# Loading half of the near table beside attention, and moving the input table's products to GpSimd, in a two-layer macaron kernel

## The chip, the cores and the metric

One core of a Trainium2 chip runs the whole program in one launch. The metric is the device time of that launch in microseconds (us). A core has TensorE (PE, with its weight loads shown apart as PEld), VectorE (DVE), ScalarE (ACT), GpSimd (POOL) and SyncE (SP, which here only issues DMAs). Each runs its own instructions in order and waits for the others by semaphores. All other data moves through 16 DMA engines.

## What is computed

x is 2048 rows of 128 numbers, f32. Six stages follow one another; `n` is a layer norm of the rows:

```python
x = x + 0.5 * moe8(n(x))                 # 8 experts, the best one for each row
x = x + windowed_attention(n(x))         # 16 heads, window of 32
x = x + 0.5 * moe8(n(x))
x = x + 0.5 * latent_block(x_normed)     # causal attention, then a moe of 4 experts
x = x + ssm(n(x))                        # state space layer
x = x + 0.5 * latent_block(x_normed)

def ssm(u):                              # D_MODEL 128, D_STATE 64, L = 2048
    K = einsum('mn,mln->ml', C_re, exp(dt[m] * A[n] * t[l]))
    return causal_convolution(u, K) + u * D

def moe(x, ...):                         # in the latent block
    top = argmax(x @ gate_w.T + gate_b)
    return (relu(x @ W1[top].T + b1[top]) @ W2[top].T + b2[top])
```

## The kernel before

The kernel is written by hand, engine by engine. The four MoE stages are numbered c = 0 to 3; c = 2 and c = 3 are those of the two latent blocks (B = 0 and B = 1), and they run the same code. "far" is True in block B = 0 alone: beside its own work it prepares the tables of the state space layer that comes next.

**A latent block.** `latent_prepare` makes keys and values. `latent_attention` runs a list of events that `plan` orders: 16 units (4 groups of 512 query rows times 4 pairs of heads); the last two units of group 3 come at places 8 and 9, those of group 2 at 10 and 11, then group 1, then group 0. `LAST[g]` is the last unit of group g. After its last unit, the group's queries (`split_q[g]`, 8 x 256 words for each partition from word 32 x 256 of `arena` on) are read no more. At the attention's end `leave_stage` drains all engines; there GpSimd scatters the 8 upper row tiles to `regions` (`scatter_routed`, one indirect DMA for each tile, L556). Then the 8 lower tiles ("late") are routed: DVE scales their rows (L1932), PE turns them (L1950), ACT copies (L1953), PE makes the gate's logits (L1957), DVE picks an expert for each row and works out its slot (`pick_dve` and `slots_dve`, a chain of small operations on 128 x 32 numbers, L410 to L441), and GpSimd scatters the 8 late tiles (L556). SP waits for all scatters to have landed, then loads 19 tiles of sorted rows (L535).

**The MoE over 19 tiles.** For each tile s, DVE copies the first layer's weights of the tile's expert to a fixed place (L661, two tiles ahead), PE multiplies (L598), ACT and DVE each make half of the hidden layer (L643 and L688), PE multiplies again (L608), DVE adds the bias (L668), and GpSimd scatters the tile's result to `made_rows` (L570). The next copy L661 waits for both halves of the tile. When all 19 have landed, SP loads the result back (L544), and the next stage's layer norm begins.

**The tables of the state space layer.** During attention of block 0, ACT and GpSimd make powers and products, PE sums them to 256 taps for each channel (event "states"), and SP writes them to `taps` in DRAM (semaphore `taps_out`, 256 when all are there). Two tables are left. `toep` (128 x 128 x 128, words 0 to 64 x 256 of `arena`, the near table) is loaded from `taps` in 8 DMAs of 1 MB (L2006), after the last row tile of the MoE has landed. `b_in` (128 x 128 x 64, words 64 x 256 to 96 x 256, where attention had its plain and shifted queries and its probabilities) is exp(-back x dt x A): in tiles s = 9 to 16 of the MoE, DVE multiplies a slice of 16 channels (128 x 1024 numbers, L1983) and ACT takes its exponential (L1998). At s = 7 ACT takes the exponentials of dt and A themselves (L1992, L1993), and DVE negates `back_col` (L1978). `state_space` reads `b_in` first, then `toep`.

## Times and profile before

| | us |
|---|---|
| three runs | 1702.85, 1703.96, 1698.28 |
| their median | 1702.85 |
| the profiled run: its time | 1704.4 |
| the profiled run: span from first to last instruction | 1703.1 |
| mean granted clock of TensorE, share of full speed | 0.847 |

| stage, in the profiled run | from, us | to, us |
|---|---|---|
| MoE of block 0 (c = 2), first hidden layer to the load back | 980.13 | 1038.36 |
| MoE of block 1 (c = 3), the same | 1648.57 | 1693.70 |

A row of the timeline has the start in us, the busy time in us, the engine, the line of the kernel, the operation, what it writes and reads, the count that was merged, and in brackets how long the engine was idle before it and who ended the idle time. Two rows with neighbouring starts may overlap a little, since an instruction is fetched while the one ahead ends. "psum" is the memory that TensorE writes, "arena" a large work area.

### The profile page before, as it was taken

The numbers are of one execution on the slowest core, as the hardware profiler recorded it, in microseconds if no ns is written. First come the engines' busy times: TensorE is split into PE (matmuls) and PEld (weight loads), VectorE is DVE, ScalarE is ACT, GpSimd is POOL, SyncE is SP. The second block draws the span as 40 slices with busy tenths as digits, with TensorE's granted clock in tenths as the row PEclk, the third lists the DMA queues.
The fourth block names the chain that finished last, engine by engine and source line by source line (L and its number), as shares of the span: only waits on it lengthen the run. The fifth ranks groups of instructions, "written<-read, shape, count | busy, mean of one in ns | idle before, by whom it ended". The sixth has DMA issues, their size and how long they took to land. (4 is left out here: it accounts for less than half of the span.)

```text
span 1703.1 us, 36518 instructions
## 1 busy us (share of the span) xinstructions
PE 1235.1 (73%) x13953; PEld 659.7 (39%) x13953; DVE 1175.8 (69%) x2641; ACT 945.3 (56%) x1507; POOL 570.0 (33%) x1034
## 2 busy tenths in 40 slices
PE   2664564447767788999997373877778999998756
PEld 2653454346542222223233273654222222233346
DVE  4348598625778989997873255476898999886234
ACT  1225775112345678878887241134566788888612
POOL 2431177045764321221112434375341111112333
PEclk9976665568579999999999596756999999999958
DMA  8410000022002100000000182000000000000022
GB/s 254 100 49 1 1 4 3 13 69 60 1 1 72 36 2 1 2 1 3 2 2 1 40 213 62 3 0 1 1 1 2 1 2 1 2 2 2 8 56 79
DMA packets 59134, 49.03 MB, mean 29 GB/s; under 512 B 7105, under 2 KB 54194, under 8 KB 58610
## 3 DMA queue, kind: packets, MB, share of 16 engines
q1 hardware_dynamic: 53282, 35.84, 7.9%
q0 software_dynamic: 4736, 9.74, 1.7%
q8 instruction: 114, 1.87, 0.5%
q10 hardware_dynamic: 944, 1.10, 0.2%
q14 instruction: 58, 0.48, 0.1%
HBM read 32.72 MB, written 18.38 MB: 30 GB/s over the span
## 5 line engine op out<-in xcount | busy, mean ns | idle before, releaser
L1808 DVE TENSOR_REDUCE arena<-psum 128x1 f32<-128x512 f32 (+4 forms) x1152 | 680.8, 656 | 138.7 <-PE psum L1619 97.6
L1751 ACT ACTIVATE arena<-psum 128x1024 f32<-128x1024 f32 (+3 forms) x640 | 558.1, 900 | 179.8 <-PE psum L1641 170.7
L1657 PE MATMUL psum<-arena 128*9 128x256 f32 (+2 forms) x4352 | 338.3, 387 | 0.9 <-POOL arena L1868 0.8
L1619 PE MATMUL psum<-arena 64*128 64x128 bf16 (+3 forms) x1664 | 223.1, 316 | 94.7 <-DVE arena L1808 87.0
L1641 PE MATMUL psum<-arena 64*128 64x512 bf16 (+3 forms) x1280 | 227.7, 356 | 23.3 <-ACT arena L1751 16.1
L1868 POOL TENSOR_SCALAR_AFFINE_SELECT arena<-arena 128x256 f32<-128x256 f32 x256 | 103.4, 408 | 367.9 <-ACT arena L1751 364.8
L1619 PEld LDWEIGHTS psum<-arena 64*128 64x128 bf16 x1664 | 69.2, 95 | 270.9 <-DVE arena L1808 233.2
L1641 PEld LDWEIGHTS psum<-arena 64*128 64x128 bf16 x1280 | 62.9, 94 | 175.9 <-ACT arena L1751 78.6
L1657 PEld LDWEIGHTS psum<-arena 128*9 128x9 f32 x4352 | 67.5, 88 | 151.8 <-issue 117.5
L1846 POOL CAST arena<-arena 128x16 bf16<-128x16 f32 x64 | 16.4, 257 | 283.9 <-DVE arena L1813 281.8
L688 DVE TENSOR_SCALAR small<-psum,YT 128x128 f32<-128x128 f32 x168 | 50.6, 343 | 77.7 <-PE psum L598 76.8
L643 ACT ACTIVATE small<-psum,YT 128x128 f32<-128x128 f32 x168 | 52.5, 364 | 84.7 <-PE psum L598 77.5
L598 PE MATMUL psum<-arena,YT 128*128 128x128 f32 x672 | 97.6, 293 | 0.1
L598 PEld LDWEIGHTS psum<-arena,YT 128*128 128x128 f32 x672 | 88.2, 205 | 3.0 <-issue 1.6
L1756 ACT ACTIVATE arena<-psum 128x1024 bf16<-128x1024 bf16 x64 | 65.4, 1024 | 33.9 <-PE psum L1605 33.3
L589 PE MATMUL psum<-ident,ACCn 128*128 128x128 f32 x16 | 7.2, 469 | 89.9 <-DMA ACCn<-sorted_rows 57.6
L570 POOL DMA_INDIRECT made_rows<-arena,index x38 | 42.5, 1120 | 77.5 <-DVE arena L668 75.8
L556 POOL DMA_INDIRECT sorted_rows<-Yn,slot x32 | 31.3, 978 | 81.3 <-DVE slot L374 72.2
L608 PE MATMUL psum<-w,small 128*128 x304 | 43.9, 290 | 15.5 <-ACT small L643 13.1
L608 PE MATMUL psum<-big_w,small 128*128 x368 | 50.9, 283 | 0.4 <-issue 0.4
L632 ACT ACTIVATE arena<-psum 128x128 f32<-128x128 f32 (+2 forms) x18 | 7.9, 444 | 77.5 <-PE psum L589 69.5
L570 POOL DMA_INDIRECT made_rows<-arena,ACCn x32 | 31.0, 968 | 56.2 <-DVE arena L668 56.2
(357 smaller groups left out, 2011.5 us busy)
## 6 DMA issues: line engine op xcount, KB each, us to landing
arena<-taps SPq DMA_DIRECT2D x8, 1024.0 KB
big_w<-in_w SPq DMA_DIRECT2D x2, 2048.0 KB, 19.3
ACCn<-made_rows SPq DMA_DIRECT2D x16, 256.0 KB, 3.8
regions<-sorted_rows SPq DMA_DIRECT2D x5, 741.8 KB, 4.6
sorted_rows<-arena SPq DMA_DIRECT2D x2, 1483.5 KB, 13.9
ACCn<-regions SPq DMA_DIRECT2D x32, 64.5 KB, 1.8
w<-in_w SPq DMA_DIRECT2D x2, 1024.0 KB
ACCn<-sorted_rows SPq DMA_DIRECT2D x6, 258.0 KB, 3.0
```

Of the source, the lines that this page charges most:

```text
L570: pool.indirect_dma_start(made_rows, bass.IndirectOffsetOnAxis(to, 0), made[q % 2][:, s % GT, :], None).then_inc(rows_made[q % 2], 16)
L598: mm = pe.matmul(hidden_of(s, k), first[s % 2][:, k * P:(k + 1) * P], xt[s // GT % 2][:, (s % GT) * P:(s % GT + 1) * P], start=True, stop= ...
L608: mm = pe.matmul(psum[:, 4 + s % 2, 0:D], hid[s % 2][:, k, :], flat2[:, bass.ds(expert[s] * HID + k * P, D)], start=(k == 0), stop=(k == H ...
L643: half = act.activation(hid[s % 2][:, k, :], hidden_of(s, k), ACT.Relu, bias=first[s % 2][:, HID + k:HID + k + 1])
L688: half = dve.tensor_scalar(hid[s % 2][:, k, :], hidden_of(s, k), first[s % 2][:, HID + k:HID + k + 1], 0.0, ALU.add, ALU.max)
L1619: mm = pe.matmul(psum[:, bank_of(("max", (v, m + r))), at:at + w], plain_q[v % 2][rows, a, i * P:(i + 1) * P], keys[rows, 2 * hq + a, key: ...
L1641: mm = pe.matmul(psum[:, b + r, off:GW], keys[rows, 2 * hq + a, t * P:(t + 1) * P], shift_q[v % 2][rows, a, off:GW], start=True, stop=True)
L1657: mm = pe.matmul(psum[32 * hh:32 * hh + 9, O_BANK, lo:hi], values[:, tile_of(v, j), 4 * hq + hh, :], prob[(t + hh // 2) % N_PROB][:, hh % ...
L1751: act.activation(prob[t % N_PROB][:, :, off:GW], both, ACT.Exp, scale=INV_SQRT_HD).then_inc(a_got, 1)
L1756: act.activation(dst, bank.bitcast(BF16).rearrange("p (a t) -> p a t", a=2), ACT.Copy).then_inc(a_got, 1)
L1808: dve.tensor_reduce(place, rows, AX.X, ALU.max).then_inc(a_max_got, 1)
L1868: pool.affine_select(out=part, in_=part, compare_op=ALU.is_ge, fill=0.0, base=0, pattern=[[0, 2], [1, P]], channel_multiplier=-1).then_inc ...
```

## The change

- **The near table.** Its upper half (channels 64 to 127, which lies where `split_q` was) is loaded beside attention in 16 DMAs of 256 KB: four for each group, from group 3 down to 0, each after a score of the group's last unit has been read. The lower half is loaded as before, in 4 DMAs of 1 MB.
- **The other table's products.** The 8 multiplications go from DVE (tiles 9 to 16) to GpSimd: two after `scatter_routed`, ahead of the late scatters, and six behind these. ACT takes the exponential of the first two behind the routing's copies, and of the other six behind tiles 1 to 6 of the MoE. The exponentials of dt and A go to the start of attention on ACT, the negation of `back_col` to its start on DVE.
- **Eight products that nobody reads.** In both blocks PE makes 8 products of 128 x 512 bf16 into a free bank of psum, ahead of turning the late rows.

```diff
+        def keep_warm(bank, n):
+            for _ in range(n):
+                pe.matmul(psum[:, bank, :].rearrange("p (a k) -> p a k", k=P), identb[:], counts[:].unsqueeze(1).broadcast_to([P, GT, P]),
+                          start=True, stop=True)
...
                     act.activation(alog_col[:], alog_col[:], ACT.Exp).then_inc(pair_made, 1)
+                    act.wait_ge(rates_in, 32)
+                    act.activation(logdt_all, logdt_all, ACT.Exp).then_inc(pair_made, 1)
+                    act.activation(alog_all, alog_all, ACT.Exp).then_inc(pair_made, 1)
...
+                if far:
+                    dve.tensor_scalar(neg_back[:], back_col[:], -1.0, None, ALU.mult).then_inc(neg_made, 1)
...
                 sp.wait_ge(taps_out, 256)
+                for g in range(NG - 1, -1, -1):
+                    for k in range(GT):
+                        sp.wait_ge(a_got, act_base + number["score", (LAST[g], k, 0)] + 1)
+                        near_table_sp(D // 2 + STEP * g + STEP // GT * k, STEP // GT)
...
+        def near_table_sp(m, n):
+            sp.dma_start(toep[:, m:m + n, :], bass.AP(tensor=taps.tensor, offset=m * 2 * P, ap=[[1, P], [2 * P, n], [1, P]])).then_inc(toep_in, 16)
+        NEAR = [slice(STEP * k, STEP * k + STEP) for k in range(D // STEP)]
+        def near_rates(k):
+            pool.wait_ge(pair_made, 4)
+            pool.wait_ge(taps_out, 256)
+            pool.tensor_tensor(b_in[:, NEAR[k], :], bcast(logdt_all[:, NEAR[k]], NS), alog_all.unsqueeze(1).broadcast_to([P, STEP, NS]),
+                               ALU.mult).then_inc(near_made, 1)
+        def near_grown(k):
+            act.wait_ge(near_made, k + 1)
+            act.wait_ge(neg_made, 1)
+            act.activation(b_in[:, NEAR[k], :], b_in[:, NEAR[k], :], ACT.Exp, scale=neg_back[:, 0:1]).then_inc(near_exp, 1)
...
             latent_attention(B, far, n, c)
+            if far:
+                for k in range(2):
+                    near_rates(k)
...
             scaled_rows(LATE)
+            keep_warm(5, 8)
...
             scatter_pool(c, 1, LATE, ACCn, regions)
+            if far:
+                for k in range(2):
+                    near_grown(k)
+                for k in range(2, D // STEP):
+                    near_rates(k)
...
-                if far and s == 7:
-                    dve.tensor_scalar(neg_back[:], back_col[:], -1.0, None, ALU.mult).then_inc(neg_made, 1)
-                    dve.wait_ge(rates_made, 3)
-                    dve.wait_ge(taps_out, 256)
-                if far and 0 <= s - 9 < D // STEP:
-                    m = STEP * (s - 9)
-                    dve.tensor_tensor(b_in[:, m:m + STEP, :], bcast(logdt_all[:, m:m + STEP], NS),
-                                      alog_all.unsqueeze(1).broadcast_to([P, STEP, NS]), ALU.mult).then_inc(near_made, 1)
...
             def beside_act(s):
-                if far and s == 7:
-                    act.wait_ge(rates_in, 32)
-                    act.activation(logdt_all, logdt_all, ACT.Exp).then_inc(rates_made, 1)
-                    act.activation(alog_all, alog_all, ACT.Exp).then_inc(rates_made, 1)
-                    act.wait_ge(neg_made, 1)
-                if far and 0 <= s - 9 < D // STEP:
-                    part = b_in[:, STEP * (s - 9):STEP * (s - 8), :]
-                    act.wait_ge(near_made, s - 8)
-                    act.activation(part, part, ACT.Exp, scale=neg_back[:, 0:1]).then_inc(near_exp, 1)
+                if far and 2 <= s + 1 < D // STEP:
+                    near_grown(s + 1)
...
                 sp.wait_ge(tile_in[CHUNKS[c] - 1], tiles_in(c, CHUNKS[c] - 1))
-                for m in range(0, D, STEP):
-                    dst, src = toep_in_of(m)
-                    sp.dma_start(dst, src).then_inc(toep_in, 16)
+                for m in range(0, D // 2, STEP):
+                    near_table_sp(m, STEP)
...
-                pe.wait_ge(toep_in, 16 * 8)
+                pe.wait_ge(toep_in, 16 * (D // 2 // STEP + NG * GT))
```

GpSimd (POOL) between attention and MoE in block 0, before: the last mask of attention, the scatters of the upper tiles, those of the late tiles, and the first rows made by the MoE.

```order
L1868 AFFINE_SELECT arena<-arena 128x2x128 [waits a_got] x13
L556 DMA regions<-ACCn,slot 8576x129 [waits slots_made,regions_in]
L556 DMA regions<-ACCn,slot 8576x129 x7
L556 DMA regions<-ACCn,slot 8576x129 [waits slots_made,stage_left]
L556 DMA regions<-ACCn,slot 8576x129 x7
L570 DMA made_rows<-arena,index 4992x128 [waits row_made,index_set]
```

The same place after; `window_mask` and `bo` are the places where dt and A lie for all partitions.

```order
L1879 AFFINE_SELECT arena<-arena 128x2x128 [waits a_got] x13
L562 DMA regions<-ACCn,slot 8576x129 [waits slots_made,regions_in]
L562 DMA regions<-ACCn,slot 8576x129 x7
L1956 TENSOR_TENSOR arena<-window_mask,bo 128x1024 [waits taps_out,pair_made,stage_left]
L1956 TENSOR_TENSOR arena<-window_mask,bo 128x1024 [waits taps_out,pair_made]
L562 DMA regions<-ACCn,slot 8576x129 [waits slots_made]
L562 DMA regions<-ACCn,slot 8576x129 x7
L1956 TENSOR_TENSOR arena<-window_mask,bo 128x1024 [waits taps_out,pair_made] x6
L576 DMA made_rows<-arena,index 4992x128 [waits row_made,index_set]
```

Two multiplications stand ahead of the late scatters, and six between these and the MoE's first scatter.

VectorE (DVE) in one of the tiles 9 to 16 of the MoE of block 0, before; L661 writes the next weights (here named by the place, YT), L688 makes half a hidden layer.

```order
L661 ISA [waits hid_act,layer1_made]
L661 COPY YT<-w 128x516
L668 ISA [waits rows_made0,layer2_made]
L668 TENSOR_TENSOR arena<-psum,arena 128x128
L1983 TENSOR_TENSOR arena<-window_mask,bo 128x1024
L688 TENSOR_SCALAR small<-psum,YT 128x128 [waits layer2_made,layer1_made]
```

The same tile after.

```order
L667 ISA [waits hid_act,layer1_made]
L667 COPY YT<-w 128x516
L674 ISA [waits rows_made0,layer2_made]
L674 TENSOR_TENSOR arena<-psum,arena 128x128
L694 TENSOR_SCALAR small<-psum,YT 128x128 [waits layer2_made,layer1_made]
```

The multiplication is gone from the tile, and nothing has come in its place.

TensorE (PE) at the end of attention in both blocks, before: the output's projection (wo), the late rows turned, and the gate.

```order
L1721 MATMUL psum<-wo,YT 128x128 x3
L1950 MATMUL psum<-ident,ACCn 128x128 [waits o_rows,stage_left]
L1950 MATMUL psum<-ident,ACCn 128x128 x3
L1950 MATMUL psum<-ident,ACCn 128x128 [waits o_rows]
L1950 MATMUL psum<-ident,ACCn 128x128 x3
L1957 MATMUL psum<-gate,YT 128x4 [waits fm_copied]
```

The same place after.

```order
L1727 MATMUL psum<-wo,YT 128x128 x3
L187 MATMUL psum<-counts,identb 128x512 [waits stage_left]
L187 MATMUL psum<-counts,identb 128x512 x7
L1988 MATMUL psum<-ident,ACCn 128x128 [waits o_rows]
L1988 MATMUL psum<-ident,ACCn 128x128 x3
L1988 MATMUL psum<-ident,ACCn 128x128 [waits o_rows]
```

The eight unread products begin as soon as the stage is left, and the turning of the late rows stands behind them.

## Rows read from the trace of the kernel before

**Rows 1.** Windows: busy us (x instructions) PE, PEld, DVE, ACT, POOL; clock; DMA; GB/s.
```profile
1005.00:1010.00 5.00, 2.19 (x18) 1.86 (x16) 3.04 (x8) 3.30 (x6) 2.77 (x2) 1.00 1.18 302
```

**Rows 2.** Timeline, ACT and SP: first hidden layer and load back, blocks 0 and 1.
```profile
980.13 0.63 ACT L643 ACTIVATE small<-psum,YT 128x128 f32<-128x128 f32 x2 [1.34 <-PE psum L598]
...
1038.36 2.01 SPq L544 DMA_DIRECT2D ACCn<-made_rows  x4
...
1648.57 0.63 ACT L643 ACTIVATE small<-psum,YT 128x128 f32<-128x128 f32 x2 [1.34 <-PE psum L598]
...
1693.70 2.03 SPq L544 DMA_DIRECT2D ACCn<-made_rows  x4
```

**Rows 3.** Timeline, DVE: one tile of block 0's MoE, then one of block 1's.
```profile
1007.69 1.22 DVE L1983 TENSOR_TENSOR arena<-window_mask,bo 128x1024 f32<-128x1024 f32 x1
...
1011.36 1.22 DVE L1983 TENSOR_TENSOR arena<-window_mask,bo 128x1024 f32<-128x1024 f32 x1
...
1675.98 0.43 DVE L661 COPY YT<-w 128x516 f32 x1 [0.84 <-PE psum L598]
...
1677.97 0.43 DVE L661 COPY YT<-w 128x516 f32 x1 [0.84 <-PE psum L598]
```

**Rows 4.** Groups by shape, POOL over the span: busy us, mean ns, idle before.
```profile
L1861 POOL TENSOR_TENSOR big_w<-big_w,c_pair 128x2064 f32<-128x2064 f32 x4 | 14.5, 3636 | 0.3
...
L774 POOL TENSOR_TENSOR arena<-arena,qk_w 128x512 f32<-128x512 f32 x4 | 7.0, 1754 | 62.2 <-DVE arena L868 62.2
...
L2028 POOL TENSOR_TENSOR X<-X,ACCn 128x2048 f32<-128x2048 f32 x1 | 4.2, 4168 | 0.1
```

**Rows 5.** Timeline, DVE and POOL between attention and MoE, block 0.
```profile
957.36 0.19 DVE L412 TENSOR_TENSOR small<-small 128x32 f32<-128x32 f32 x1
957.59 0.19 DVE L413 TENSOR_TENSOR small<-small,order 128x32 f32<-128x32 f32 x1
...
959.48 0.17 DVE L441 CAST slot<-small 128x8 uint32<-128x8 f32 x1
...
981.65 0.43 DVE L661 COPY YT<-w 128x516 f32 x1 [0.84 <-DVE small L688]
...
960.43 0.96 POOL L556 DMA_INDIRECT regions<-ACCn,slot  x1 [5.01 <-DVE slot L441]
...
984.92 0.96 POOL L570 DMA_INDIRECT made_rows<-arena,index  x1 [14.57 <-DVE arena L668]
```

**Rows 6.** Timeline, POOL and DVE at once, in windowed attention and after the state space.
```profile
270.27 1.27 POOL L1034 TENSOR_TENSOR arena<-arena 128x512 f32<-128x512 f32 x1
...
270.58 1.50 DVE L1003 TENSOR_TENSOR arena<-arena 128x512 f32<-128x512 f32 x1
...
1094.73 0.98 POOL L1513 MEMSET arena<- 128x1024 bf16 x1
1094.81 0.92 DVE L1473 TENSOR_SCALAR scales<-meanvar 128x4 f32<-128x4 f32 x1
```

**Rows 7.** Timeline of PE, three places, and a window in the columns of rows 1.
```profile
526.51 1.04 PE L1605 MATMUL psum<-identb,arena 128*128 128x128 bf16 x8
...
910.86 1.28 PE L1711 MATMUL psum<-gate,YT 128*128 128x4 f32 x10
...
1620.26 1.94 PE L1950 MATMUL psum<-ident,ACCn 128*128 128x128 f32 x8 [4.14 <-DVE ACCn L1932]
1622.12 3.57 PE L1957 MATMUL psum<-gate,YT 128*128 128x4 f32 x16
...
1646.62 3.62 PE L598 MATMUL psum<-arena,YT 128*128 128x128 f32 x16
...
1648.00:1653.00 5.00, 5.00 (x29) 5.00 (x29) 2.26 (x8) 1.26 (x4) 0.00 (x0) 0.58 0.25 63
```

**Rows 8.** Timeline, ACT: the exponential of dt, and block 1's first step after attention.
```profile
997.36 0.31 ACT L1992 ACTIVATE window_mask<-window_mask 128x128 f32<-128x128 f32 x1
...
1618.76 0.21 ACT L1943 ACTIVATE rstd<-rstd 128x8 f32<-128x8 f32 x1 [0.52 <-ACTq L177]
```

2 lines of the change are left out of this document (removed).

## The prediction, made before the changed kernel was run

> **What bounds the kernel now.** No engine is the bound throughout, so I read the two MoE stages of the latent blocks side by side. They run the same code on 19 tiles, except that the first also prepares the state space layer's tables. From the first hidden layer to the load back, block 0 takes 1038.36 - 980.13 = 58.2 us and block 1 takes 1693.70 - 1648.57 = 45.1 us [rows 2]. The table work costs 13.1 us there. The timeline of DVE tells where: with a multiplication L1983 (1.22 us) in it, a tile lasts 1011.36 - 1007.69 = 3.67 us, in block 1 1677.97 - 1675.98 = 1.99 us [rows 3]. Eight such tiles differ by 8 x 1.68 = 13.4 us, which is the whole 13.1. The multiplication explains 1.2 of the 1.7; the rest is that ACT's exponential waits for it, and the next weight copy waits for ACT. It isn't TensorE: in such a stretch it is busy 2.19 of 5 us at clock 1.00 [rows 1].
>
> **The tiles lose the multiplications: -13.1 us.** What block 1 takes is what block 0 should take without table work on DVE. The DMAs are not in it: in the same window they move 302 GB/s [rows 1], and no tile's 3.67 us is more than its DVE and ACT work explains. The DMA half that stays (4 MB, 14 us at that rate) is issued where the whole was, and is in long before the stage ends; the half beside attention is issued by SP, which has nothing else to do there, and DMAs take no engine's time. I cost both at 0. If a transfer were late, PE would wait for it ahead of the near products; of that there is no sign.
>
> **Six exponentials stay on ACT, in tiles 1 to 6: +0.2.** Of the new tiles' period of 2 us, the two activations L643 take 0.63 [rows 2], an exponential at most 1.22, L1983's time for the same width [rows 3]. 1.85 fits. In tiles 2 and 6 ACT also copies the next rows and may overrun a period a little. The first two exponentials fall where ACT has nothing to do. The negation on DVE is one tiny operation, and is costed at 0.
>
> **Two exponentials at attention's start: +0.35.** The first ACT copy there waits behind them. That of dt takes 0.31 [rows 8], but the next begins 0.2 after its start; the other is smaller. Bounds 0 (if PE was late anyway) and 0.5.
>
> **The price of a multiplication on GpSimd** isn't in the trace, so it is bounded: 3636 / 2064 x 1024 = 1.8 us by L1861, 1754 x 2 = 3.5 us by L774, which goes in runs of 8 elements; by L2028, 4168 / 2 = 2.1 us [rows 4]. The new one has runs of 64, nearer to L1861 and L2028. I take 2.0. The Trainium skill (GPSIMD Engine Reference, section on elementwise cycle accounting) has 4497 ns for 2048 elements, an estimate of 2.25 us for ours; the sum below would be about 1.2 us worse by it, and the row of this kernel decides.
>
> **Two multiplications ahead of the late scatters: +2.2.** GpSimd is idle for 5.01 us before the first late scatter at 960.43 [rows 5], so since 955.42. The two run to about 955.6 + 2 x 2.05 = 959.7, and the slots come at 959.48 + 0.17 = 959.65. By this alone they just fit. But DVE's routing runs at the same time, and rows 6 show what happens then: DVE's L1003 begins at 270.58 with GpSimd's L1034 running until 270.27 + 1.27 = 271.54, and takes 1.50 us, though its 512 columns at L1983's rate (1024 in 1.22) need about 0.6. So it waited for the end of GpSimd's instruction, and then went ahead of GpSimd's next one. In the routing L412 (957.36) and L413 (957.59) both read two operands from SBUF, as L1003 does [rows 5]. L412 would wait until 957.65, L413 behind the second multiplication until 959.75. From L413 to the slots it is 959.65 - 957.59 = 2.06, so the slots come at 961.8, late by 2.2. All that follows (scatters, landing, loads, MoE) moves by it. Bounds: 0 without such waiting, +3.1 at 2.5 us each. What PE adds ahead of L412 in this block (below) is covered up to 1.4 us, since L412 would be waiting then anyway.
>
> The Trainium skill (SBUF — State Buffer, section on the two separate sides) states the same as a rule: DVE and GpSimd share one pair of ports, held by one instruction at a time, against DVE operations in a 2-port mode or with two inputs from SBUF. It speaks against placing these products beside the routing; hanging on it are the +2.2 and the +1.0 below, and without both the sum would be -12.4.
>
> **Six multiplications behind the late scatters: +1.0.** Today these scatters end at 984.92 - 14.57 = 970.35 [rows 5]; now 972.6. Six more take until 972.6 + 6 x 2.05 = 984.9. The MoE's own first GpSimd scatter is due at 984.92 + 2.2 = 987.1, so no row waits. DVE's third weight copy L661 is due at 981.65 + 2.2 = 983.9 [rows 5], while the last multiplication runs. A DVE operation with one input waits too: L1473, four numbers, took 0.92 us beside a GpSimd memset that began at 1094.73 and lasted 0.98 [rows 6]. The copy waits some 1.0 us, and since DVE paces these tiles, that stays. Bounds 0 and 2.8 (at 2.5 us each, two or three waits).
>
> **Eight unread products: +0.1 in block 1, nothing more in block 0.** PE is free once the stage is left, just before 1618.76, when ACT gets its release [rows 8]: say 1618.55. Today it waits until 1620.26 for the scaled rows [rows 7]. Eight bf16 products of 128 columns took 1.04 us at the lower level [rows 7], about 0.11 each; ours have 512 columns, 0.44 each, 3.5 in all, until 1622.05. The turning is late by 1.8. Against this stands the clock. From 1646.62 on PE multiplies densely (16 x L598 in 3.62 us), and the mean of 0.58 in 1648 to 1653 says that the clock went from half (1.2 GHz) to full (2.4 GHz) near 1652.2, so 5.6 us later [rows 7]. Counted from 1618.55 that is 1624.1, when the gate's 16 products L1957 would just begin. They took 3.57 us at half; ten of the same shape took 1.28 at full (L1711), so 16 take 1.9 [rows 7]: 1.7 us back. Net +0.1. Bounds -0.5 (the clock rises earlier) and +1.8 (it doesn't rise in time).
>
> **The sum.** -13.1 + 0.2 + 0.35 + 2.2 + 1.0 + 0.1 = -9.25 us. The profiled run took 1704.4, so it would be 1695.2. The median of the three runs is 1702.85 (1698.28 to 1703.96); less 9.25 it gives 1693.6, my forecast.
>
> **The rivals.**
> - *No waiting between DVE and GpSimd.* The routing's operations are very short, and the copy may come between two products. Then 2.2 and 1.0 go: -12.4, 1690.4. Rows 6 speak against it.
> - *The unread products only delay.* The clock rises by what PE did before, and the turning is all that follows them; the gate's products have 4 columns. Then +1.8 in block 1 instead of +0.1; block 0 hides most of it. -7.5, 1695.3. Speaks for it: the margin between 1624.1 and the end of dense work is nil.
> - *GpSimd is slower, 2.5 us each:* the routing costs 3.1, the MoE 2.8. -6.5, 1696.3.
> - *Slower than before: GpSimd's products last into the MoE.* At 3.5 us each (L774's price) the two cost the routing 2 x 3.55 - 1.9 = 5.2, and the six end at 975.6 + 21.3 = 996.9, while the MoE starts its hidden layers at 985.3. If DVE gets nothing done in those 11.6 us, the sum is -13.1 + 0.2 + 0.35 + 5.2 + 11.6 + 1.8 = +6, 1708.9. With x for the price it is about 8x - 22.2 in this worst case, so it decides from x = 2.8 on.
> - *The change doesn't do what it says:* block 1 is no measure, since something else (the load's traffic, or the exponentials in the early tiles) holds the tiles, and half the gain stays away: -9.25 + 6.5 = -2.7, 1700.1.
>
> **How the numbers follow.** Forecast 0.50; no waiting 0.14; unread products only delay 0.17; slower GpSimd 0.09; half the gain 0.05; slower 0.05. The range goes from below the first rival (1689.5) to 1699.5, above the cases of -7.5 and -6.5 with room for the before runs, whose own spread is 5.7 us; it leaves out half the gain and the slower case, and the tails. 0.3% is 5.1 us, about what a measurement of this kernel can tell from no change. The first four cases, 0.90, lie beyond it, but the two smaller gains by little, so I give faster 0.83, within 0.3% 0.13, slower 0.04.
>
> **What would show it.** In the profile after: block 0's stage near 46.5 us; tiles 9 to 16 at 2.0 us on DVE; the product on GpSimd near 2.0; L412 and L413 of the routing (with new line numbers) longer than 0.19, and the late scatters some 7.2 us behind the earlier ones' end instead of 5.0; one weight copy of DVE near the MoE's start longer than 0.43; the gate's 16 products in block 1 near 1.9 us, or 3.6 if the clock didn't rise. Wrong it would be if tiles 9 to 16 stayed above 2.5 us, or a wait for `toep_in` or `near_exp` showed up in the state space stage.

## The result: faster by 0.83%, more than forecast

| | before | after |
|---|---|---|
| median, us (8 runs each) | 1702.13 | 1690.65 |
| lowest and highest, us | 1698.28, 1708.98 | 1685.82, 1692.31 |
| ratio of the runs, 95% interval | | 0.9917 (0.9902 to 0.9933) |

By the ratio the change takes off 14.1 us (11.4 to 16.7), where 9.25 were forecast; the difference of the medians is 11.5. Three later controls gave ratios of 0.9920, 0.9925 and 0.9891. The kernel is faster, as forecast, but by more than the sum said, and by the ratio more than the range allowed (from 1702.85 it reached down to 1689.5, so 13.35 us).

The profiled run after took 1690.99 us (span 1689.7). First both MoE stages, ACT and SP, the rows that answer to [rows 2]:

```profile
986.07 0.63 ACT L649 ACTIVATE small<-psum,YT 128x128 f32<-128x128 f32 x2 [1.34 <-PE psum L604]
...
1030.69 2.01 SPq L550 DMA_DIRECT2D ACCn<-made_rows  x4
...
1635.96 0.63 ACT L649 ACTIVATE small<-psum,YT 128x128 f32<-128x128 f32 x2 [1.34 <-PE psum L604]
...
1680.72 2.03 SPq L550 DMA_DIRECT2D ACCn<-made_rows  x4
```

Block 0's MoE takes 1030.69 - 986.07 = 44.6 us instead of 58.2, and block 1's 44.8. DVE in two tiles of block 0, at the place of [rows 3]: the multiplication is gone and a tile lasts 1006.77 - 1004.78 = 1.99 us.

```profile
1004.78 0.43 DVE L667 COPY YT<-w 128x516 f32 x1 [0.85 <-ACT small L649]
1005.13 0.28 DVE L674 TENSOR_TENSOR arena<-psum,arena 128x128 f32<-128x128 f32 x1
1005.33 0.60 DVE L694 TENSOR_SCALAR small<-psum,YT 128x128 f32<-128x128 f32 x2
1006.77 0.43 DVE L667 COPY YT<-w 128x516 f32 x1 [0.84 <-PE psum L604]
```

Between attention and MoE of block 0, DVE and GpSimd (POOL), at the place of [rows 5]:

```profile
959.13 0.96 POOL L562 DMA_INDIRECT regions<-ACCn,slot  x1 [0.30 <-issue]
959.56 0.19 DVE L416 TENSOR_TENSOR small<-psum,gateb 128x32 f32<-128x32 f32 x1 [3.69 <-PE psum L1995]
959.78 0.19 DVE L417 TENSOR_REDUCE small<-small 128x8 f32<-128x32 f32 x1
960.00 3.93 DVE L418 TENSOR_TENSOR small<-small 128x32 f32<-128x32 f32 x1
960.11 3.76 POOL L1956 TENSOR_TENSOR arena<-window_mask,bo 128x1024 f32<-128x1024 f32 x2
...
963.97 0.19 DVE L419 TENSOR_TENSOR small<-small,order 128x32 f32<-128x32 f32 x1
...
966.31 1.01 POOL L562 DMA_INDIRECT regions<-ACCn,slot  x1 [2.43 <-DVE slot L447]
...
976.38 11.18 POOL L1956 TENSOR_TENSOR arena<-window_mask,bo 128x1024 f32<-128x1024 f32 x6
...
987.60 0.43 DVE L667 COPY YT<-w 128x516 f32 x1 [0.84 <-DVE small L694]
```

L418 (L412 before) takes 3.93 us instead of 0.19: it ends when both multiplications have ended, at 963.87. The next one, L419, waits for nothing. From the end of the last upper scatter (959.13 + 0.96 = 960.09) to the first late one it is 6.22 us, where it was 5.01. A multiplication takes 11.18 / 6 = 1.86 us. The six end at 987.56, and DVE's third weight copy comes at 987.60 and takes 0.43.

TensorE in block 1's routing, and the two exponentials at attention's start on ACT, which answer to [rows 7] and [rows 8]:

```profile
1606.54 3.52 PE L187 MATMUL psum<-counts,identb 128*128 128x512 bf16 x8 [2.20 <-ACTq L177]
1609.89 1.04 PE L1988 MATMUL psum<-ident,ACCn 128*128 128x128 f32 x8
1611.28 1.95 PE L1995 MATMUL psum<-gate,YT 128*128 128x4 f32 x16 [0.34 <-ACT YT L1991]
```

```profile
492.15 0.29 ACT L1747 ACTIVATE window_mask<-window_mask 128x128 f32<-128x128 f32 x1
492.35 0.24 ACT L1748 ACTIVATE bo<-bo 128x64 f32<-128x64 f32 x1
492.50 1.00 ACT L1765 ACTIVATE arena<-psum 128x1024 bf16<-128x1024 bf16 x1
```

After the unread products the turning takes 1.04 us instead of 1.94 and the gate's products 1.95 instead of 3.57.

One profile each doesn't settle where the gain lies, since stages with the same code differ between executions too. With the experiments' controls there are three profiles of the kernel before and four of the changed one. The borders are: ACT's first exponential at attention's start (L1738 before, L1744 after), ACT's square root for the late rows (L1943, L1980), the first hidden layer, and the load back.

| stage | before, mean (range) | after, mean (range) | difference |
|---|---|---|---|
| ahead of attention of block 0 | 491.0 (489.6 to 492.8) | 491.3 (489.9 to 493.6) | +0.3 |
| attention of block 0 | 459.5 (458.2 to 461.3) | 461.0 (458.9 to 462.3) | +1.5 |
| routing of block 0 | 30.75 (30.55 to 31.05) | 31.85 (31.19 to 32.34) | +1.1 |
| MoE of block 0 | 58.33 (58.22 to 58.55) | 44.78 (44.49 to 45.31) | -13.55 |
| load back of block 0 to late routing of block 1 | 580.42 (580.40 to 580.46) | 578.62 (576.33 to 579.99) | -1.8 |
| routing of block 1 | 29.79 (29.76 to 29.81) | 29.05 (28.94 to 29.24) | -0.74 |
| MoE of block 1 | 45.05 | 44.89 | -0.2 |
| the rest | 9.8 | 9.1 | -0.7 |
| span | 1704.7 | 1690.6 | -14.0 |

The MoE and the routing of block 0, the routing of block 1, and attention's first copy (+0.3) give -12.9 us. The rest of attention, beside which the 16 DMAs now run, is not in this sum: its +1.5 is less than what it varies in one kernel (458.2 to 461.3 before).

### The profile page after: what moved, and what is told of

Its sections match the earlier page's. It is cut to its first block and busy times, and to the rows that moved or that the text cites. A ratio compares the mean times of both kernels' runs of the same rounds, so it can differ in the third digit from the quotient of the medians.

```text
span 1689.7 us, 36574 instructions
## 1 busy us (share of the span) xinstructions
PE 1233.8 (73%) x13969; PEld 655.1 (39%) x13969; DVE 1169.9 (69%) x2633; ACT 945.2 (56%) x1507; POOL 578.8 (34%) x1042
## 5 line engine op out<-in xcount | busy, mean ns | idle before, releaser
L694 DVE TENSOR_SCALAR small<-psum,YT 128x128 f32<-128x128 f32 x168 | 50.5, 342 | 77.4 <-PE psum L604 76.6
L604 PE MATMUL psum<-arena,YT 128*128 128x128 f32 x672 | 97.3, 293 | 0.7 <-issue 0.6
L604 PEld LDWEIGHTS psum<-arena,YT 128*128 128x128 f32 x672 | 87.6, 205 | 4.5 <-issue 2.7
L576 POOL DMA_INDIRECT made_rows<-arena,index x38 | 37.6, 990 | 57.1 <-DVE arena L674 54.9
L614 PE MATMUL psum<-big_w,small 128*128 x368 | 51.0, 283 | 0.5 <-issue 0.5
L667 DVE COPY YT<-big_w 128x516 f32 x46 | 21.2, 461 | 39.4 <-PE psum L604 27.1
```

Source lines behind the costliest of these rows:

```text
L576: pool.indirect_dma_start(made_rows, bass.IndirectOffsetOnAxis(to, 0), made[q % 2][:, s % GT, :], None).then_inc(rows_made[q % 2], 16)
L604: mm = pe.matmul(hidden_of(s, k), first[s % 2][:, k * P:(k + 1) * P], xt[s // GT % 2][:, (s % GT) * P:(s % GT + 1) * P], start=True, stop= ...
L614: mm = pe.matmul(psum[:, 4 + s % 2, 0:D], hid[s % 2][:, k, :], flat2[:, bass.ds(expert[s] * HID + k * P, D)], start=(k == 0), stop=(k == H ...
L694: half = dve.tensor_scalar(hid[s % 2][:, k, :], hidden_of(s, k), first[s % 2][:, HID + k:HID + k + 1], 0.0, ALU.add, ALU.max)
```

## The experiments

**Theory:** the gain is the multiplications' move off DVE; against it stands the routing's wait behind GpSimd; the DMAs are free; the unread products bring the clock up earlier. **Rivals:** the early DMAs or the moved exponentials carry part of the gain; the routing isn't held by GpSimd; the unread products only delay. A ratio below is that to the kernel before on the same chip, with its 95% interval.

### Three controls

The changed kernel twice and the kernel before once, unedited.

> The changed kernel once more, as a control for the others and for stages whose code is the same in both kernels. In the two profiles shown, the part from block 0's load back to block 1's first step after attention, whose instructions are identical, takes 580.40 us before and 576.33 after. Theory (the clock's steps fall elsewhere in each execution): here the same part takes some other value between 573 and 583 us, the time differs from the first profile's, and the stages that the change touches repeat: routing of block 0 about 32.3 us, MoE of block 0 about 44.6 us, DVE's second-operand instruction L418 again near 3.9 us. Rival (the change itself makes the later part faster, by what it leaves in memory or queues): the part takes 576.3 again within 0.5 us.

> The kernel before once more. Its first profile had 580.40 us from block 0's load back to block 1's first step after attention, while five profiles of changed kernels have 579.02, 579.02, 579.04, 578.82 and 576.33 us with the same instructions there. Theory (this part differs by where the clock's steps fall, not by the change): a value between 576 and 582, not systematically above 579; MoE of block 0 again 58.2 us, routing of block 0 30.5, of block 1 29.8. Rival (the change makes that part shorter by 1.4 us in each execution): 580.4 again.

> The changed kernel once more, beside the two that follow, so that they can be compared on one chip. Stages of the two profiles before: routing of block 0 32.34 and 32.00 us, MoE of block 0 44.62 and 44.71, routing of block 1 28.94 and 29.07. Expected: the same within 0.4 us, DVE's L418 between 1.9 and 3.95 us long, by when it comes in the row of two multiplications.

Measured: 1691.27 us, 0.9920 (0.9901 to 0.9939), and 1691.67 us, 0.9925 (0.9912 to 0.9938), for the changed kernel; 1706.16 us, 1.0002 (0.9991 to 1.0013), for the one before. The touched stages repeat (table above). The wait is there again, but shorter than the 3.9 us that I had expected, since DVE comes later in the row of two, in after_again:

```profile
956.18 0.19 DVE L416 TENSOR_TENSOR small<-psum,gateb 128x32 f32<-128x32 f32 x1 [5.17 <-PE psum L1995]
956.41 0.19 DVE L417 TENSOR_REDUCE small<-small 128x8 f32<-128x32 f32 x1
956.63 1.99 DVE L418 TENSOR_TENSOR small<-small 128x32 f32<-128x32 f32 x1
...
954.78 3.77 POOL L1956 TENSOR_TENSOR arena<-window_mask,bo 128x1024 f32<-128x1024 f32 x2
```

The first multiplication ends at 954.78 + 1.88 = 956.66. DVE asks at 956.63, 0.03 us ahead of that, and still waits until the second has ended. So close to the border that alone proves little; but in after_third L418 starts at 958.96, 0.9 us ahead of the border, and ends at 961.82 with the second (958.00 + 3.76 = 961.76). L417, a reduction with one input from SBUF, takes its 0.19 us in the midst of the row.

### The multiplications back on DVE in tiles 9 to 16 (tiles_on_dve)

```diff
-                for k in range(2):
-                    near_rates(k)          # GpSimd, ahead of the late scatters
...
-                for k in range(2, D // STEP):
-                    near_rates(k)          # GpSimd, behind them
...
+                if far and 0 <= s - 9 < D // STEP:
+                    near_rates(s - 9)      # on DVE, in tile s
```

> The changed kernel with the eight multiplications back on DVE in tiles 9 to 16 of the MoE, the exponentials behind them as before; the exponentials of dt and A at attention's start, half of the near table beside attention and the unread products stay as changed. Theory (the gain is the multiplications' move alone): MoE of block 0 58.2 us (tiles at 3.67), routing of block 0 30.5 us, so 13.6 - 1.5 = 12 us slower than the changed kernel and within 1 us of the kernel before. Rival (part of the 13.6 us is from the DMAs moved out of the MoE, or from the exponentials of dt and A moved out): MoE at 52 to 57 us.

Measured: MoE of block 0 58.47 us, routing of block 0 31.09, routing of block 1 29.14; 1704.77 us, 0.9993 (0.9981 to 1.0005). All of the MoE's gain is gone, though half of the near table still comes beside attention and the exponentials of dt and A are still early. DVE at the place of [rows 3]:

```profile
1012.44 0.43 DVE L667 COPY YT<-w 128x516 f32 x1 [1.38 <-ACT small L649]
1012.78 0.28 DVE L674 TENSOR_TENSOR arena<-psum,arena 128x128 f32<-128x128 f32 x1
1012.98 1.22 DVE L1956 TENSOR_TENSOR arena<-window_mask,bo 128x1024 f32<-128x1024 f32 x1
1014.12 0.61 DVE L694 TENSOR_SCALAR small<-psum,YT 128x128 f32<-128x128 f32 x2
1016.11 0.43 DVE L667 COPY YT<-w 128x516 f32 x1 [1.38 <-ACT small L649]
```

A tile is 3.67 us again. The early DMAs alone gain nothing.

### The whole near table loaded in the MoE (table_whole)

```diff
-                for g in range(NG - 1, -1, -1):
-                    for k in range(GT):
-                        sp.wait_ge(a_got, ...)
-                        near_table_sp(D // 2 + STEP * g + STEP // GT * k, STEP // GT)
...
-                for m in range(0, D // 2, STEP):
+                for m in range(0, D, STEP):
```

> The changed kernel with the whole near table loaded in the MoE, as before, and nothing of it beside attention. In the kernel before, eight DMAs kept 300 GB/s up for 27 us from about 998 on, and ended 11 us ahead of the load back. In the changed kernel the load back comes 13.6 us sooner, so the eight would end about when it begins, 1 to 2 us behind it. Theory (the split is worth nothing on its own and 1 to 3 us once the MoE is short): attention the same, MoE tiles at 2.0 to 2.1 us as in the changed kernel, MoE of block 0 44.7 us, and 1 to 3 us more from the load back to the states' products, since the loaded rows land later. Rival (the prediction's 0 for all of it): no stage differs by more than 0.5 us. Rival (the split disturbs attention or the whole load slows the MoE's tiles): attention shorter by over 1 us than 458.3 us, or tiles above 2.2 us.

Measured: MoE of block 0 47.58 us, 3.1 more than after_third on the same chip (44.49), all tiles alike (first to last 38.95 us against 38.91), attention the same (462.3 both, so the 16 DMAs beside it cost nothing there); 1693.99 us, 0.9935 (0.9920 to 0.9949). By the timed runs alone this isn't to be told from the changed kernel; the stage is. The end of the MoE on GpSimd, whose last scatter of results must land ahead of the load back, here and in after_third:

```profile
1028.55 0.96 POOL L576 DMA_INDIRECT made_rows<-arena,index  x1 [0.30 <-issue]
1033.88 0.21 POOL L2041 MEMSET arena<- 128x64 f32 x1 [4.37 <-DMA made_rows<-arena,index]
```

```profile
1026.24 0.95 POOL L576 DMA_INDIRECT made_rows<-arena,index  x1 [0.30 <-issue]
1028.53 0.21 POOL L2046 MEMSET arena<- 128x64 f32 x1 [1.33 <-DMA made_rows<-arena,index]
```

The wait for the landing is 4.37 us with the table and 1.33 without, 3.04 more, which is the 3.1. Windows of table_whole in the columns of rows 1 show the table still moving there, at 320 and 294 GB/s:

```profile
1027.00:1030.00 3.00, 0.26 (x3) 0.07 (x1) 0.29 (x1) 0.23 (x1) 1.92 (x2) 1.00 1.15 320
1030.00:1033.00 3.00, 0.00 (x0) 0.00 (x0) 0.00 (x0) 1.06 (x1) 0.00 (x0) 0.90 1.02 294
```

So the theory had the cost right and the place wrong: not the loaded rows, but the last results land late. The split is worth 0 in the long MoE (tiles_on_dve) and 3.0 us in the short one. The Trainium skill (DMA: Bandwidth & Descriptors, section on queues, rings and completion order) says that a DMA engine takes its queues in turn, packet by packet. The landing that comes 3 us later, while another queue is busy, agrees in direction; how the turns fall no run here shows.

### Without the unread products (no_unread)

```diff
-            keep_warm(5, 8)
```

> The changed kernel without the eight unread products, in both blocks. Theory: they are worth 0.9 us in block 1's routing (28.94 us with them, 29.81 in the kernel before), and nothing in block 0, where DVE's L418 waits until 963.9 for GpSimd whatever TensorE does; so slower by about 0.9 us, the gate's 16 products of block 1 at 3.6 us instead of 1.95, and block 0's routing at 32.3 as with them. Rival (they only delay the turning): faster by 1.8 us. Rival (they bring the clock up in block 0 as well, which matters): slower by 2.5 us.

Measured: routing of block 1 29.76 us, of block 0 32.07, 1693.91 us, 0.9929 (0.9910 to 0.9947). TensorE in block 1:

```profile
1607.01 1.94 PE L1987 MATMUL psum<-ident,ACCn 128*128 128x128 f32 x8 [4.13 <-DVE ACCn L1966]
1608.87 3.57 PE L1994 MATMUL psum<-gate,YT 128*128 128x4 f32 x16
```

Block 1 loses 0.7 us, as in the kernel before; block 0 is as in after_again (32.00). The rival that they only delay falls. The timed runs can't tell 0.7 us.

### All eight multiplications behind the late scatters (all_behind), and the same with waits (behind_apart)

```diff
-            if far:
-                for k in range(2):
-                    near_rates(k)
...
-                for k in range(2, D // STEP):
+                for k in range(D // STEP):
+                    if k:                            # behind_apart alone
+                        pool.wait_ge(near_made, k)   # behind_apart alone
                     near_rates(k)
```

> The changed kernel with all eight multiplications on GpSimd behind the late scatters, none ahead. Theory (L418's 3.93 us was its wait for both multiplications, and the whole routing waited with it): the late scatters start about 3.7 us earlier after the earlier ones' end, the routing of block 0 takes 28.6 us instead of 32.3. The eight then run for 8 x 1.87 = 15 us and end some 5 us after the MoE's first hidden layer. If DVE waits for the whole row of multiplications, its third weight copy loses 3.8 us and the sum is 0; if it comes in between two of them, two copies or so lose 1 us each, and the sum is -2. Rival (the routing wasn't held by that wait): no gain in the routing, and 1 to 4 us slower in all.

> As the run with all eight multiplications on GpSimd behind the late scatters, but GpSimd waits for each multiplication's own semaphore before it starts the next. There DVE's third weight copy took 4.00 us, to the end of the last multiplication, and the MoE 50.4 us. Theory (a row of GpSimd multiplications that follow each other without a wait keeps DVE out as a whole; a wait between them lets DVE in): no DVE instruction waits longer than 2.0 us, the third weight copy takes 0.4 to 2.3 us, the MoE of block 0 46 to 48 us, so 2.5 to 4 us faster than that run and about as fast as the changed kernel or 1 us better. Rival (DVE is kept out as long as GpSimd has multiplications, wait or not): the copy again takes until the last one ends, MoE 50.4.

Measured for all_behind: routing 29.89 us, MoE 50.40; 1693.44 us, 0.9927 (0.9911 to 0.9942). For behind_apart: routing 30.94, MoE 47.41; 1693.64 us, 0.9925 (0.9907 to 0.9943). From DVE's first routing step (L416) to the first late scatter it is 3.5 us in both, as in the kernel before; with two multiplications ahead it is 6.75, 4.81, 5.69 and 4.57 us in the four profiles of the changed kernel. So the wait does hold the routing, though without it the routing took 29.89 us and not the 28.6 expected. all_behind, DVE beside the row of eight:

```profile
973.06 14.91 POOL L1956 TENSOR_TENSOR arena<-window_mask,bo 128x1024 f32<-128x1024 f32 x8
...
982.80 0.61 DVE L694 TENSOR_SCALAR small<-psum,YT 128x128 f32<-128x128 f32 x2 [13.12 <-PE psum L604]
984.25 4.00 DVE L667 COPY YT<-w 128x516 f32 x1 [0.84 <-DVE small L694]
```

behind_apart, the same place:

```profile
972.94 15.83 POOL L1956 TENSOR_TENSOR arena<-window_mask,bo 128x1024 f32<-128x1024 f32 x8
...
984.15 0.89 DVE L667 COPY YT<-w 128x516 f32 x1 [0.84 <-PE psum L604]
984.95 1.86 DVE L683 COPY_PREDICATED index<-valid,ACCn 128x4 uint32<-128x4 uint32 x1
```

The copy L667 waits 3.6 us, until the last of the row ends at 987.97. With GpSimd waiting for its own semaphore between two multiplications (0.13 us each: (15.83 - 14.91) / 7), the copy comes in after at most one, and nothing takes longer than 1.86. The theory of the row holds, with a limit: no wait in these runs goes past more than one border between two multiplications, so that a longer row holds DVE to its end isn't shown. L694, which reads psum, takes its 0.61 us beside the multiplications in both. Neither version wins: against the changed kernel's means all_behind gains 2.0 us in the routing and loses 5.6 in the MoE, behind_apart gains 0.9 and loses 2.6.

The 5.6 us are more than the wait of 3.6. TensorE has nothing to do meanwhile (3.19 us idle), and when it goes on its granted clock is at half (a window in the columns of rows 1):

```profile
988.30:992.10 3.80, 3.75 (x17) 3.78 (x18) 1.99 (x8) 0.63 (x2) 1.01 (x1) 0.50 0.23 53
```

Eight products L614 ahead of the idle time took 1.06 us; eight L604 behind it take 2.05, in after_again 1.06 at a granted clock of 1.00 (983.30 to 987.40). By the starts of DVE's half of the hidden layer, the second and third tile together last 2.1 us longer than in after_again, which is the rest.

### The multiplications in DVE's idle time (gap_on_dve, gap_three, gap_three_four)

DVE is idle for 13 us between the routing's tables and the first hidden layer (the 13.12 in brackets in all_behind's rows). GpSimd issues a tiny memset behind its last late scatter, on whose semaphore DVE starts:

```diff
+                pool.memset(scattered_mark[:], 0.0).then_inc(pair_made, 1)
+                for k in range(NEAR_EARLY):          # 6; 3 in gap_three
+                    near_grown(k)
...
+            def ahead_dve():                         # called behind the first two weight copies
+                for k in range(D // STEP):
+                    near_rates(k)                    # on DVE, waits for pair_made 5
...
-            keep_warm(5, 8)
+            keep_warm(5, 4)                          # gap_three_four and gap_four_second alone
```

> The changed kernel with all eight multiplications on DVE, in its 13 us of idle time between the routing's tables and the first hidden layer, behind a mark that GpSimd sets after its last late scatter; six exponentials follow at once on ACT, two go into tiles 1 and 2 of the MoE. Theory: the late scatters start 3.7 us earlier, eight multiplications at 1.22 to 1.24 us take 9.9 us, from the mark at about 972.5 to 982.4, and the first hidden layer is due at about 982.4: 3.7 us faster than the changed kernel, routing 28.6 us, MoE 44.6. Rival (the routing wasn't held by the wait): no difference. Rival (DVE's multiplications last into the MoE): 1 to 2 us of the 3.7 are lost.

> As the run with the multiplications in DVE's idle time, but with three of the exponentials ahead of the MoE's row copies on ACT instead of six, five in tiles 1 to 5. There the routing took 31.85 us, 1.1 more than pick at 7.34 us and late scatters 3.5 us behind it would give, and ACT's first row copy came at +28.9 us of it instead of +25.5, behind the sixth exponential. Theory (ACT's row copies waited for the exponentials): first row copy at +25.5, routing 30.5 us, MoE 44.6 to 44.9, so 1.3 us faster than that run and 1.5 us faster than the changed kernel. Rival (something else holds the first hidden layer, as the loads of the sorted rows): routing stays at 31.8.

> The run with the multiplications in DVE's idle time and three exponentials ahead of the MoE's copies, with four unread products in each block in place of eight. In block 1 eight took 3.5 us at half clock and put the turning off from +1.50 to +2.86 us behind ACT's step, while the gate's 16 products fell from 3.57 to 1.95 us; the pick came at +6.22 instead of +6.97. Theory (four end at about +1.3, ahead of the scaled rows, and put nothing off; the clock has then risen or not): if it has risen when the gate's products come, pick at +5.4 to +5.8 in block 1, 0.5 to 0.8 us sooner than with eight; if not, at +6.97, 0.75 us later. I expect the latter in one of two executions, so no difference in the time. Block 0: routing 30.1 to 30.6 us, MoE 44.6 to 44.9; about 1.5 us faster than the changed kernel on the same chip.

gap_on_dve: routing 31.85 us, MoE 44.48; 1689.74 us, 0.9908 (0.9891 to 0.9925). gap_three: routing 30.11, MoE 44.60; 1690.49 us, 0.9922 (0.9899 to 0.9944). gap_three_four: 30.11, 44.27, and 28.33 in block 1's routing; 1686.22 us, 0.9887 (0.9873 to 0.9902), beside 0.9925 of the changed kernel on the same chip. The routing of 28.6 us that I expected of gap_on_dve didn't come, and gap_three's 1.5 us over the changed kernel can't be told in its time. DVE and ACT in gap_on_dve:

```profile
971.28 9.17 DVE L1961 TENSOR_TENSOR arena<-window_mask,bo 128x1024 f32<-128x1024 f32 x8 [3.50 <-POOL scattered_mark L2005]
972.54 6.82 ACT L1967 ACTIVATE arena<-arena,neg_back 128x1024 f32<-128x1024 f32 x6 [15.88 <-DVE arena L1961]
...
979.27 0.60 ACT L641 ACTIVATE arena<-psum,norm_w 128x128 f32<-128x128 f32 x2
```

Eight multiplications take 9.17 us and end at 980.45, ahead of the first hidden layer. But ACT's first row copy stands behind the sixth exponential. With three ahead of it, the copy comes in time (gap_three):

```profile
972.96 3.42 ACT L1967 ACTIVATE arena<-arena,neg_back 128x1024 f32<-128x1024 f32 x3 [14.99 <-issue]
976.40 0.37 ACT L641 ACTIVATE arena<-psum,norm_w 128x128 f32<-128x128 f32 x1
```

Four unread products, in block 1 of gap_three_four:

```profile
1606.53 1.89 PE L187 MATMUL psum<-counts,identb 128*128 128x512 bf16 x4 [2.20 <-ACTq L177]
1608.41 1.73 PE L1989 MATMUL psum<-ident,ACCn 128*128 128x128 f32 x8
1610.31 1.95 PE L1996 MATMUL psum<-gate,YT 128*128 128x4 f32 x16 [0.17 <-ACT YT L1992]
```

They put nothing off, and the gate's products still run at 1.95 us. I had expected that in one of two executions. In block 0 of the same execution it went the other way: the four ran at full clock, and the gate's products behind them at half.

```profile
953.15 1.04 PE L187 MATMUL psum<-counts,identb 128*128 128x512 bf16 x4 [2.20 <-ACTq L177]
...
956.95 3.58 PE L1996 MATMUL psum<-gate,YT 128*128 128x4 f32 x16
```

The granted clock there is 0.50 from 955 to 960.6. So four are not enough everywhere.

### Once more, for what was open

before_third and after_fourth are the two kernels, gap_three_second and gap_four_second the last two versions, all unedited.

> The kernel before, for the part with identical instructions. Theory (it differs by where the clock's steps fall, and two values of 580.4 were chance): below 580.0 or above 580.9. Rival (the change shortens it by 1.4 us or more): 580.4 within 0.4. The touched stages: routing of block 0 30.5 to 31.1 us, MoE of block 0 58.2 to 58.6, routing of block 1 29.8.

> The changed kernel, control for this chip. The part with identical instructions took 576.33, 579.02 and 579.14 us; theory (the clock's steps): any value between 576 and 581; rival (shortened by the change): 579.1 or below. Touched stages: 32.0, 44.6, 29.0 us.

> Multiplications in DVE's idle time, three exponentials ahead of the MoE's copies, eight unread products. Routing of block 0 30.1 us against 32.0, MoE 44.6: 1.9 us faster than the changed kernel by the stages. The first time the timed runs showed 0.9922 against 0.992 and 0.9925 of the changed kernel, thus nothing, with one run of 1699.6 among six. Theory (the stages are right, that comparison was across chips): 1.5 to 2.5 us faster than after_fourth. Rival (the gain is given back later): the same time as after_fourth.

> The same with four unread products in each block. Its first profile had block 1's pick at +5.29 us behind ACT's step instead of +6.22 and the routing at 28.33 us instead of 29.0. Theory (four end ahead of the scaled rows, put nothing off and still bring the clock up): block 1's pick again at +5.3 to +5.6, 0.7 us faster than gap_three_second, 2.5 to 3.5 us faster than after_fourth. Rival (it was that execution's luck where the clock stepped): pick at +6.9, no faster than gap_three_second.

| | median, us | ratio (95% interval) | routing 0 | MoE 0 | routing 1 |
|---|---|---|---|---|---|
| before_third | 1705.56 | 0.9996 (0.9982 to 1.0011) | 30.66 | 58.22 | 29.76 |
| after_fourth | 1688.54 | 0.9891 (0.9867 to 0.9916) | 31.19 | 45.31 | 29.24 |
| gap_three_second | 1690.87 | 0.9904 (0.9885 to 0.9923) | 30.77 | 45.92 | 29.65 |
| gap_four_second | 1689.08 | 0.9893 (0.9873 to 0.9913) | 30.73 | 45.10 | 28.13 |

Block 1's routing with four products repeats (28.33, 28.13; with eight 28.94 to 30.45 in eleven profiles; without 29.76 to 29.81 in four): DVE's first step (the "pick" of the expectations) comes 5.29 us behind ACT's both times, instead of 6.21 to 6.58 and 6.97 to 7.13. So four are worth 1.5 us in block 1, in two of two profiles, and eight 0.7 in the changed kernel (0.5 over all eleven). In time the version with four beats the changed kernel on one chip (by 5.5 us of the medians) and not on the other; by the three stages it is 2.6 and 1.8 us faster. gap_three_second missed its expectation: 1.5 to 2.5 us faster than after_fourth, it came out 2.3 us slower by the medians and 0.6 by the three stages. gap_four_second was to be 2.5 to 3.5 us faster and was 0.5 slower by the medians. That it beats both kernels is shown against the kernel before, and only likely against the changed one.

The part with identical instructions took 580.46 us in before_third and 579.99 in after_fourth. Three profiles before lie within 0.06 us, and all fourteen of changed kernels below them (576.33 to 579.99). before_again (580.41) and before_third are where the rival had them; after_fourth is above the 579.1 that it wanted. So the rival, that something shortens this part a little, has more for it than my theory of chance, but less than three equal numbers suggest: before_again is 4.0 us behind the first profile from 194 to 525 us into the part (by the same copies of ACT) and has made it all up by the end. No run names the cause: it stays without the unread products (579.02), with the whole table in the MoE (579.38) and with the multiplications back on DVE (577.37).

## Why the prediction was right in kind and too small in size

The cause was right: the gain is the multiplications' move off DVE, and GpSimd's take a part of it back. Three steps of the sum failed, all to the same side. The wait ahead of the late scatters was put at +2.2 and cost +1.1. The wait of the third weight copy was put at +1.0 and didn't come, by a margin of 0.04 us. The unread products were put at +0.1 and gave 0.74 back, since the clock was already up for the turning, and not only for the gate's products. Against each step, the means of the table:

- **Tiles lose the multiplications, -13.1.** Right, and the largest term: tiles_on_dve returns it whole. With the next two steps the forecast for the stage was -11.9; it was -13.55. Tiles 9 to 16 together went from 29.3 us (before) to 16.7 (after_again), by the starts of DVE's half of the hidden layer; the other 1.0 lies in the first tiles and the stage's end. Of the 1.65 us that the stage gained beyond the forecast 1.0 is the copy's wait below and 0.2 the exponentials; the last 0.45 is within what the stage varies (44.49 to 45.31).
- **The DMAs at 0.** The sum's 0 came out only because the table was split. Block 1, my measure for the tiles, has no table load, so its 45.1 us hold no landing behind one; the step asked whether PE waits for the table, and not who waits behind it once the MoE ends 13 us sooner. Without the split 3.0 of the 13.55 stay away (table_whole).
- **Exponentials in tiles, +0.2:** about nothing; tiles 1 to 6 last as long as in block 1.
- **Two exponentials at attention's start, +0.35:** right for the copy. The copy started 490.88 - 490.61 = 0.27 us behind the first exponential before, and starts 492.50 - 491.90 = 0.60 behind it now.
- **A multiplication at 2.0:** 1.86. The row nearest to it (1.8 by L1861, [rows 4]) was the better guess. The estimate of 2.25 us by the Trainium skill (GPSIMD Engine Reference, section on elementwise cycle accounting) is 21% above what was measured.
- **Ahead of the late scatters, +2.2:** DVE did wait, but the mechanism was half right. I had L412 wait for the first multiplication and L413 for the second, as L1003 came in between two GpSimd instructions in [rows 6]. Here one instruction waited for both. What I had not read in the code: a self-wait of GpSimd stands between L1034 and the next (`own_pool`), and behind_apart shows that such a wait lets DVE in. The price from L416 to the scatter is 3.2 us in the first profile and 1.05 to 2.2 in the others (mean 1.9), by how much of the row is left when DVE asks. But it is the row's end that counts: the first late scatter starts 6.22 or 6.23 us behind the end of the last upper one in all six profiles with two multiplications there, no_unread and table_whole among them, where 7.2 was forecast and 5.0 was before. Of the missing 1.0 about half is the row itself, which is over 3.78 us behind the upper scatters instead of 4.3; the other half is that the scatter follows the slots after 0.28 us instead of 0.78, for which no run shows the reason. That DVE's first routing step comes 0.95 us sooner than before (on average 6.6 against 7.5 us behind ACT's step) is lost in the same wait. In the stage it is +1.1.
- **The third weight copy, +1.0:** nothing. The six end at 987.56 and the copy comes at 987.60; in after_again at 982.25 and 982.32. At the forecast's price of 2.05 it would have waited. The margin is 0.04 to 0.20 us in the six profiles, so it is luck and not a rule; all_behind shows the 3.6 us that it costs without it.
- **Unread products, +0.1:** -0.74 in block 1. The delay was 1.36 us (turning from +1.50 to +2.86 behind ACT's step) instead of 1.8, and the gate's gain was as forecast (3.57 to 1.95). What failed is the time of the clock's rise: the step took it from the MoE, 5.6 us behind the first product, when the turning is over. Here the turning starts 1609.89 - 1606.54 = 3.35 us behind the first product and runs at full clock: 1.94 to 1.04, another 0.9. Some 0.4 of it is lost again, since the gate now waits for ACT's copy (0.34 in brackets): 1.36 - 0.90 + 0.42 - 1.62 = -0.74. The windows of the profile after have the granted clock at 0.50 (1.2 GHz) under the unread products and at 0.95, near 2.4 GHz, right behind them:

```profile
1606.50:1609.50 3.00, 2.96 (x7) 1.03 (x8) 2.23 (x10) 0.21 (x1) 2.39 (x3) 0.50 0.49 116
1609.50:1613.00 3.50, 3.16 (x26) 2.75 (x24) 0.00 (x0) 1.26 (x2) 0.09 (x1) 0.95 0.09 32
```

So -1.65 in the MoE, -1.1 in the routing of block 0 and -0.85 in block 1's: 3.6 us more than -9.25 makes -12.9. The last 1.1 us to the -14.0 of the spans are a sum of differences that nothing here explains: +0.3 ahead of attention and +1.2 in the rest of attention, both of which vary by up to 4 us from one execution to the next, -0.9 at the end, and the -1.8 of the long part between the blocks.

Of the rivals, "no waiting between DVE and GpSimd" (-12.4) was nearest in time and wrong in cause: the wait is there and makes one instruction 3.9 us long. That its number fits is luck.

**Open besides.** In block 0, DVE's first routing step starts 0.03 to 2.14 us after the gate's last product (0.39 to 0.89 in the three profiles of the kernel before), and in the longest cases the profile names no engine, as in behind_apart, where the gate's products end at 957.46:

```profile
959.50 0.19 DVE L416 TENSOR_TENSOR small<-psum,gateb 128x32 f32<-128x32 f32 x1 [5.67 <-remote]
```

In block 1 it is 0.03 to 0.05 us. Where it is long, it takes away what the clock gains in block 0 (in behind_apart the gate ends 1.2 us sooner than in the kernel before and DVE starts 0.5 us later); no run was made on it.

## What to carry to other kernels

When work leaves a stage, the stage ends sooner, and a transfer that was hidden in it must be priced anew against what has to land at its end. Two multiplications on GpSimd that follow each other without a wait act on DVE as one long instruction, and a wait of DVE that leaves TensorE idle can cost its clock as well: put them where DVE has nothing to do, break the row with a wait, or use DVE's own idle time. Filler work for the clock should end before the work that it serves is ready; in block 1 half of it was worth twice as much. It must be tried at each place, since in block 0 the same half once left the gate at half clock.

## What the runs showed of the hardware

- A DVE instruction that has to wait for GpSimd isn't let in at the border between two back-to-back instructions (3.93 us for two, 3.6 us for the last two of eight, 2.86 us when it asks 0.9 us ahead of the border); a semaphore wait of 0.13 us between them is enough to let it in. Waits past more than one border weren't seen. The Trainium skill (SBUF — State Buffer, section on the two separate sides) has the shared pair of ports held for one whole instruction. The rows agree that it isn't shared, and go further: between two instructions without a wait it wasn't handed over.
- A copy with one input from SBUF (L667) and a copy by mask (L683) wait like operations with two inputs. One input from psum (L694, 0.61 us) doesn't, and neither does a reduction with one input from SBUF (L417, 0.19 us).
- With a table moving at some 300 GB/s in SP's queue, the last scatter from GpSimd's landed 3.0 us later (a wait of 4.37 us instead of 1.33).
- After 3.19 us without work behind a waiting copy, TensorE's granted clock was 0.50 (1.2 GHz), and the next eight products took 2.05 us instead of 1.06.
- The multiplication with operands of 64 repeated elements takes 1.86 us on GpSimd and 9.17 / 8 = 1.15 us on DVE.
